# Attention values folded after the sum instead of before it, GpSimd rounding x, and a theta copy by DMA

## The reference, cut to what matters

```python
# B=16 images, C=256 channels, HW=1024 pixels
theta = theta_w @ x                     # 32 rows, 1024 pixels
phi   = pool2(phi_w @ x)                # 2x2 maximum: 32 rows, 256 places
beta  = softmax(theta^T phi, axis=-1)   # 1024 x 256
g     = pool2(g_w @ x)                  # 128 rows, 256 places
o     = o_w @ (g @ beta^T)              # 256 x 1024
y     = gamma * o + x
out   = y + tpl @ y                     # tpl: 27 taps along the channels, circular
```

## Time and profile before

| | |
|---|---|
| Three runs, median | 288.54 us |
| The profiled execution: time, span | 288.93 us, 287.2 us |
| PE busy | 276.3 us (96%) |
| DVE, ACT, POOL busy | 238.0, 235.1, 117.7 us |
| DMA (queue of SP) | 53.1% of 16 engines |
| granted clock, mean | 0.994 |

### The profile page before, as it was taken

The page is one execution under the profiler, slowest core; times in us unless marked ns, Lnnn a source line. Parts: engine busy times, 40 slices in busy tenths (PEclk is TensorE's granted clock), DMA queues, the critical chain, the costliest instruction groups (busy, mean ns, idle before and its releaser), DMA issues.

```text
span 287.2 us, 4324 instructions
## 1 busy us (share of the span) xinstructions
PE 276.3 (96%) x1276; PEld 222.7 (78%) x1276; DVE 238.0 (83%) x401; ACT 235.1 (82%) x519; POOL 117.7 (41%) x59
## 2 busy tenths in 40 slices
PE   5878999999999999999999999999999999999995
PEld 3556778888887888888788888878888887888884
DVE  4897979888897988889798888979888897988750
ACT  1799797997979799797979989797998979799762
POOL 7056336335433633543363353345335334533200
PEclk9799999999999999999999999999999999999999
DMA  7633628193662818466281846628184662818033
GB/s 223 189 53 55 193 119 217 46 243 141 191 193 112 200 71 235 146 192 189 116 224 41 235 146 192 189 118 203 61 238 143 192 189 119 217 46 235 0 149 146
DMA packets 12647, 44.57 MB, mean 155 GB/s; under 512 B 2063, under 2 KB 2653, under 8 KB 11390
## 3 DMA queue, kind: packets, MB, share of 16 engines
q1 hardware_dynamic: 12252, 44.13, 53.1%
q10 hardware_dynamic: 274, 0.20, 0.2%
q0 software_dynamic: 112, 0.13, 0.1%
HBM read 17.37 MB, written 16.78 MB: 119 GB/s over the span
## 4 chain that ended last, share of the span: by engine, by line
PE 87%; DVE 6%; ACT 3%; DMA 2%; issue 1%; POOLq 0%
PE psV L666 15%; PE psV L667 14%; PE psV L668 14%; PE psY L693 10%; PE psY L666 6%; PE psY L667 6%; PE psY L668 6%; PE psV L779 4%; PE psX L746 3%; PE psZ L746 2%; PE psX L732 2%; PE psZ L732 2%; DMA taps_sb<-taps 2%; PE psY L779 1%; DVE theta_aug L513 1%; DVE neg_max L559 1%
## 5 line engine op out<-in xcount | busy, mean ns | idle before, releaser
L324 POOL TENSOR_TENSOR prob_lo<-prob,prob_hi 128x1024 fp32r<-128x1024 f32 x30 | 72.2, 2405 | 94.3 <-ACT prob_hi L396 94.3
L318 POOL TENSOR_TENSOR x_lo<-x_raw,x_hi 128x1024 fp32r<-128x1024 f32 x15 | 36.1, 2409 | 51.5 <-DVE x_hi L490 42.8
L382 ACT ACTIVATE psX<-psX,neg_max 128x256 f32<-128x256 f32 x64 | 28.6, 447 | 25.9 <-DVE neg_max L559 25.7
L369 ACT CAST theta_aug<-thetaphi 32x512 fp32r<-32x512 f32 x64 | 39.6, 618 | 1.2
L666 PE MATMUL psV<-prob_hi,value_hi 128*128 128x512 f32 x94 | 37.8, 403 | 0.0
L668 PE MATMUL psV<-prob_hi,value_lo 128*128 128x512 f32 x94 | 37.2, 395 | 0.0
L667 PE MATMUL psV<-prob_lo,value_hi 128*128 128x512 f32 x94 | 36.9, 393 | 0.0
L507 DVE TENSOR_TENSOR thetaphi<-psY,thetaphi_rest 64x512 f32<-64x512 f32 x32 | 21.8, 683 | 11.4 <-ACT thetaphi_rest L363 11.4
L382 ACT ACTIVATE psZ<-psZ,neg_max 128x256 f32<-128x256 f32 x64 | 29.6, 482 | 0.4 <-DVE neg_max L559 0.4
L513 DVE TENSOR_TENSOR theta_aug<-thetaphi,theta_aug 32x512 fp32r<-32x512 f32 x32 | 26.1, 818 | 1.0
L408 ACT COPY y<-psV 128x512 f32<-128x512 f32 x31 | 18.5, 596 | 9.1 <-PE psV L668 9.1
(11 more groups left out here) (127 smaller groups left out, 723.2 us busy)
## 6 DMA issues: line engine op xcount, KB each, us to landing
x_raw<-x SPq DMA_DIRECT2D x15, 1024.0 KB, 5.5
out<-y SPq DMA_DIRECT2D x15, 1024.0 KB, 4.0
x_edge<-x_hi SPq DMA_DIRECT2D x64, 104.0 KB
x_edge<-x_lo SPq DMA_DIRECT2D x32, 104.0 KB
x_raw<-x SPq DMA_DIRECT2D x4, 256.0 KB, 4.6
out<-y SPq DMA_DIRECT2D x4, 256.0 KB, 2.0
band_rev<-ring SPq DMA_DIRECT2D x2, 128.0 KB, 4.0
proj_raw<-proj_wT ACTq DMA_DIRECT2D x1, 192.0 KB, 3.9
```

What stands on the lines that cost most here:

```text
L318: nc.gpsimd.tensor_tensor(x_lo[:, par, :, cols], x_raw[:, par, :, cols], x_hi[:, par, :, cols].bitcast(F32), ALU.subtract).then_inc(x_lo_r ...
L324: nc.gpsimd.tensor_tensor(prob_lo[:, h], prob[:, h], prob_hi[:, h].bitcast(F32), ALU.subtract).then_inc(prob_lo_ready, 1)
L369: nc.scalar.copy(theta_aug[rows, par, h * HALF:(h + 1) * HALF], thetaphi[0:K, h, :]).then_inc(theta_hi_ready, 1)
L382: last = nc.scalar.activation(tiles[:, t, :], tiles[:, t, :], ACT.Exp, bias=neg_max[:, col:col + 1], accum_out=exp_sum[:, col:col + 1])
```

## The change

For image n, `attention_input(h)` now multiplies the pooled g, turned (g transposed, `gT`), by `prob` into one bank: `o_in` (6 matmuls a half). ACT (half 0) and DVE (half 1) round `o_in` to its high part, DVE makes its low part, and `add_high_attention` and `add_low_attention` multiply by W2's parts (3 matmuls for each of four output banks). g is turned by `g_transposed`: two float32 matmuls of 128 columns against the unit matrix, in place of `values`; ACT and DVE split the result, 256 columns instead of 512. DVE's `split_g` goes. POOL rounds both halves of x. Theta's second high copy is a DMA on SP (`copy_theta_high`), ahead of the x load, and the edge transfers now come behind that load. The taps are fetched by ACT's queue, ahead of the weights, and not by POOL's. Ten idle matmuls stand at the start instead of eight. Banks are reassigned, and with them waits. ("..." marks lines left out.)

```diff
-        g_hi = sb("g_hi", [P, M], F32R)
-        g_lo = sb("g_lo", [P, M], F32R)
-        value_hi = sb("value_hi", [P, 2, MT, C], F32R)
-        value_lo = sb("value_lo", [P, 2, MT, C], F32R)
+        gT_hi = sb("gT_hi", [P, MT, CG], F32R)
+        gT_lo = sb("gT_lo", [P, MT, CG], F32R)
+        o_in_hi = sb("o_in_hi", [P, 2, HALF], F32R)
+        o_in_lo = sb("o_in_lo", [P, 2, HALF], F32R)
...
         psV = ctx.enter_context(nc.psum_tensor("psV", [P, 2, HALF], F32))
         scores_ps = [psX, psZ]
-        thetaphi_ps = [psY[:, 0, :], psY[:, 1, :]]
-        second_thetaphi_ps = [psY[:, 1, :], psY[:, 0, :]]
-        g_ps = [psV[:, 0, :], psY[:, 0, :]]
-        value_ps = psV[:, 1, :]
-        out_ps = [[psV[:, 1, :], psV[:, 0, :]], [psY[:, 1, :], psV[:, 0, :]]]
-        last_out_ps = [out_ps[0], [psY[:, 1, :], psY[:, 0, :]]]
-        w2_ps = psV[:, 1, 0:C]
+        turn_ps = [psV[:, 0, :], psV[:, 1, :]]
+        shared_ps = psY[:, 1, :]
+        g_o_in_ps = psY[:, 0, :]
+        w2_ps = psY[:, 1, 0:C]
...
         def is_second(i, par):
             return is_number(i) and i == 0 and par == 1

-        def thetaphi_bank(i, par, h):
-            return (second_thetaphi_ps if is_second(i, par) else thetaphi_ps)[h]
+        def thetaphi_bank(par, h):
+            return turn_ps[par] if h == 0 else shared_ps
+
+        def g_bank(par, h):
+            return g_o_in_ps if h == 0 else turn_ps[par]
+
+        def gT_bank(i, par):
+            bank = turn_ps[0] if is_first(i, par) else turn_ps[1 - par]
+            return bank[:, 0:M]
+
+        def o_in_bank(i, par, h):
+            if is_last(i, par):
+                return scores_ps[h][:, 0, :]
+            return shared_ps if h == 0 else g_o_in_ps
+
+        def out_bank(i, par, h, f):
+            if f == 0:
+                return turn_ps[par if h == 0 else 1 - par]
+            return g_o_in_ps if h == 1 and is_last(i, par) else shared_ps
...
+            def copy_theta_high(i, par, h):
+                sp.wait_ge(theta_hi_ready, upto(2, i, par, h + 1))
+                cols = slice(h * HALF, (h + 1) * HALF)
+                sp.dma_start(theta_aug[K:2 * K, par, cols].bitcast(F32),
+                             theta_aug[0:K, par, cols].bitcast(F32)).then_inc(theta_copied[h], 16)
...
+            hi, lo = (b[:, :, :].rearrange("p t c -> p (t c)")[:, P:P + CT * P] for b in (band_hi, band_lo))
+            sp.wait_ge(band_parts_ready, 1)
+            stack_edges(edge_w[:, :], edge_w_loaded, (hi, hi))
...
-            stack_edges(edge_w[:, :], edge_w_loaded, (hi, hi, lo))
+            stack_edges(edge_w[:, :], edge_w_loaded, (lo,), 2)
...
                 if has_next(i, par):
-                    x_edges(*following(i, par))
+                    for h in range(2):
+                        copy_theta_high(*following(i, par), h)
...
                     load(i + 1, par)
                 if has_next(i, par):
+                    x_edges(*following(i, par))
...
-            pool.dma_start(taps_sb[:], taps).then_inc(taps_loaded, 16)
...
+            def x_high(i, par, h):
+                cols = slice(h * HALF, (h + 1) * HALF)
+                pool.wait_ge(x_loaded[par], 16 * (i + par))
+                pool.wait_ge(x_used, upto(2, i, par, h - 3))
+                pool.sem_inc(x_buffer_free, 1)
+                nc.gpsimd.tensor_copy(x_hi[:, par, :, cols], x_raw[:, par, :, cols]).then_inc(x_hi_ready[h], 1)
...
-                    for h in range(2):
-                        prob_low(i, par, h)
+                    prob_low(i, par, 0)
+                    pool.wait_ge(theta_lo_ready, upto(2, *following(i, par), 2))
+                    prob_low(i, par, 1)
                 if has_next_but_one(i, par):
+                    x_high(i + 1, par, 0)
                     x_low_of_half_0(i + 1, par)
+                    x_high(i + 1, par, 1)
...
+            act.dma_start(taps_sb[:], taps).then_inc(taps_loaded, 16)
...
-                for rows in (slice(0, K), slice(K, 2 * K)):
-                    nc.scalar.copy(theta_aug[rows, par, h * HALF:(h + 1) * HALF],
-                                   thetaphi[0:K, h, :]).then_inc(theta_hi_ready, 1)
+                cols = slice(h * HALF, (h + 1) * HALF)
+                nc.scalar.copy(theta_aug[0:K, par, cols], thetaphi[0:K, h, :]).then_inc(theta_hi_ready, 1)
+                if is_first(i, par):
+                    nc.scalar.copy(theta_aug[K:2 * K, par, cols], thetaphi[0:K, h, :]).then_inc(first_theta_copy_ready, 1)
...
+            def gT_high(i, par):
+                act.wait_ge(gT_done, upto(1, i, par, 1))
+                nc.scalar.copy(gT_hi[:], gT_bank(i, par).rearrange("p (t c) -> p t c", t=MT)).then_inc(gT_hi_ready, 1)
+
+            def o_in_high(i, par, h):
+                act.wait_ge(o_in_done, upto(2, i, par, h + 1))
+                nc.scalar.copy(o_in_hi[:, h], o_in_bank(i, par, h)).then_inc(o_in_hi_ready[h], 1)
...
+                o_in_high(i, par, 0)
                 if ahead:
                     exp_sums(ni, npar, 0)
+                else:
+                    o_in_high(i, par, 1)
...
                     ln_sums(ni, npar)
+                    gT_high(ni, npar)
                 out_of_psum(i, par, 1, 0)
-                if ahead:
-                    value_high(ni, npar)
-                if has_next_but_one(i, par):
-                    x_high(i + 1, par, 1)
...
-            def x_high(i, par, h):
...
+                pool2(g_pool[:, h * MH:(h + 1) * MH], g_bank(par, h)).then_inc(g_pooled, 1)
+
+            def gT_low(i, par):
+                dve.wait_ge(gT_hi_ready, upto(1, i, par, 1))
+                nc.vector.tensor_tensor(gT_lo[:], gT_bank(i, par).rearrange("p (t c) -> p t c", t=MT),
+                                        gT_hi[:].bitcast(F32), ALU.subtract).then_inc(gT_lo_ready, 1)
+
+            def o_in_high(i, par, h):
+                dve.wait_ge(o_in_done, upto(2, i, par, h + 1))
+                nc.vector.tensor_copy(o_in_hi[:, h], o_in_bank(i, par, h)).then_inc(o_in_hi_ready[h], 1)
+
+            def o_in_low(i, par, h):
+                dve.wait_ge(o_in_hi_ready[h], upto(1, i, par, 1))
+                nc.vector.tensor_tensor(o_in_lo[:, h], o_in_bank(i, par, h), o_in_hi[:, h].bitcast(F32),
+                                        ALU.subtract).then_inc(o_in_lo_ready[h], 1)
...
-                if has_next_but_one(i, par):
-                    x_high(i + 1, par, 0)
+                o_in_high(i, par, 1)
+                o_in_low(i, par, 1)
                 shifts(ni, npar)
+                gT_low(ni, npar)
...
+            def g_transposed(i, par):
+
+                if not is_first(i, par):
                     pe.wait_ge(out_evacuated[0][0], upto(1, i, par, 0))
-                pe.wait_ge(g_lo_ready, upto(1, i, par, 1))
+                pe.wait_ge(g_pooled, upto(2, i, par, 2))
                 for t in range(MT):
                     tile = slice(t * P, (t + 1) * P)
-                    last = three(value_ps[:, t * C:(t + 1) * C], (g_hi[:, tile], g_lo[:, tile]),
-                                 (w2_hi[:], w2_lo[:]), True, True)
-                last.then_inc(value_done, 1)
+                    last = nc.tensor.matmul(gT_bank(i, par)[:, tile], g_pool[:, tile], ident[:], start=True, stop=True)
+                last.then_inc(gT_done, 1)
...
+                    pe.wait_ge(theta_copied[h], 16 * upto(1, i, par, 0))
...
-                    pe.wait_ge(value_lo_ready, upto(1, i, par, 1))
+                    pe.wait_ge(gT_lo_ready, 1)
+                elif (h, f) == (0, 0):
+                    pe.wait_ge(out_evacuated[1][0], upto(1, i, par, 0))
                 elif (h, f) == (0, 1):
                     if has_next(i, par):
-                        pe.wait_ge(g_pooled, upto(2, *following(i, par), 1))
+                        pe.wait_ge(o_in_lo_ready[0], upto(1, i, par, 1))
...
                     if has_next(i, par):
-                        pe.wait_ge(thetaphi_summed, upto(2, *following(i, par), 1 if is_first(i, par) else 2))
+                        pe.wait_ge(g_pooled, upto(2, *following(i, par), 2))
...
+            def attention_input(i, par, h):
+
+                if h == 0 and has_next(i, par):
+                    pe.wait_ge(thetaphi_summed, upto(2, *following(i, par), 2))
+                elif has_next(i, par):
+                    pe.wait_ge(g_pooled, upto(2, *following(i, par), 1))
+                bank = o_in_bank(i, par, h)
+                pe.wait_ge(gT_lo_ready, upto(1, i, par, 1))
+                pe.wait_ge(prob_hi_ready, upto(2, i, par, h + 1))
+                for t in range(MT):
+                    for g_part in (gT_hi, gT_lo):
+                        nc.tensor.matmul(bank, g_part[:, t, :], prob_hi[:, h, t, :],
+                                         start=t == 0 and g_part is gT_hi, stop=False)
                 pe.wait_ge(prob_lo_ready, upto(2, i, par, h + 1))
+                for t in range(MT):
```

(67 more changed lines are left out.)

115 lines of the change are left out of this document (49 added, 66 removed).

## The result

The changed kernel takes 291.25 us (median of 7 runs, 290.07 to 293.21), the kernel before, on the same chip, 288.6 (7 runs, 288.28 to 289.33). The ratio is 1.0093, 95% interval 1.007 to 1.0116: slower, by more than the 0.3% that can be told. The forecast was 290.1 with a range of 286.6 to 293.0, and slower was given 0.55. The profiled execution took 291.25, with a span of 289.3 (before: 288.93 and 287.2).

What follows compares the result with a forecast made beforehand. PE's work bounded the kernel before; DVE's path to `o_in_low` was to set the changed body. 288.93 - 1.9 (start) + 0.2 (first body) + 3.3 (middle) = 290.5, less 0.39 for the median: 290.1 us, range 286.6 to 293.0.

Steps and rivals of the forecast that it cites:

- The middle: Each of 14 bodies: PE waits for DVE's `o_in_low`; body 16.97 us, 0.23 more than before, 3.3 in all; chance 0.52.
- if PE shows no idle time in the middle: Sign that the prediction is wrong: it expected PE idle ahead of the filter group, ending with DVE's `o_in_low`.
- What was late next: End of a body: shift rows ready at 16.6 to 17.0, level with PE's coming at 16.97 and next to be late.
- Turning g: Two float32 matmuls of 128 columns on PE in each body: 0.43 us, at most 0.88.
- What is hidden: Work off PE in each body: ACT's and DVE's changes, the theta transfer and POOL's rounding were to cost no time.
- The theta transfer: Theta's second high copy by DMA: 2.1 us, landing before the scores; rival at 4.0 is late, 299 us, chance 0.06.
- POOL's rounding: Rounding of x on POOL: 1.1 us, hidden up to 2.0; rival that it takes 2.4, 294.3 us, chance 0.07.
- The first body: First body, 16.04 us before: the longer DVE queue makes it 0.2 longer.
- The last: Last body: same number of matmuls, new waits inside other work, so a change of 0.
- The start: Work ahead of the middle: weights, maximum and PE clock together 1.9 us earlier (0.9 to 2.4).
- the weights' 1.2: Start: weights split 1.2 us earlier with the taps first on ACT's queue, 0.5 if they take the taps' 4.6.
- The maximum moved ahead: Start: the maximum of psZ goes ahead of a pooling, so the exponential no longer waits for it: 0.4 us.

Runs made afterwards that it cites:

- e1: The changed kernel with two high additions of `o_in` put between the two halves' scores on PE: 286.34 us, ratio 0.9923.
- e7: The changed kernel with DVE's pooling of g moved from ahead of theta's first low part to between the two maxima: 287.15 us, ratio 0.9937.
- e2: The changed kernel with `o_in_low` of half 0 put ahead of theta's second low part on DVE: 300.21 us, ratio 1.0401.
- e9: The changed kernel with DVE's pooling of g moved behind `o_in_low` and ahead of both maxima: 291.2 us, ratio 1.0088.
- e4: The kernel before with only the start's edits, taps first on ACT's queue and ten idle matmuls: 288.24 us, ratio 0.9982.
- e10: e1 with the pooling of g also moved between the two maxima, as in e7: 284.15 us, ratio 0.9856.
- e3: The changed kernel with theta's second high copy made by ACT again in place of the DMA: 298.31 us, ratio 1.0333.
- e6: e1 with x's high parts rounded by DVE (half 0) and ACT (half 1) again, not by POOL: 286.77 us, ratio 0.9933.

## Why the prediction was right, point by point

**The middle: right, for the reason given.** The body was put at 16.97 and is 16.94; the filter group at 9.35 and it starts at 9.32 (149.42 - 140.10); the psZ scores at 8.6, and they start at 8.64; theta's first low part at 6.1 with 0.68, and it stands at 6.07 with 0.68. The three experiments on this path moved the body as its terms say: cover (e1, 16.65), a shorter queue (e7, 16.66), theta's low part behind `o_in_low` (e2, 17.43). With both repairs the body is 16.47, which is the sum that the prediction gave for PE alone, and 0.27 less than before. So the arithmetic of the change does save what was computed, 14 x 0.27 = 3.8 us, and in the order in which it came a wait of 0.47 a body took it all and 2.8 more. Two things it had wrong. One of its signs of being wrong, "if PE shows no idle time in the middle", came true by its words: PE's rows show none there, only the distances and the weight loads do, so it was the sign that was badly chosen. And it left out 0.08 ahead of the psX scores, which changed nothing, since the psZ scores wait behind them.

**What was late next: right.** Shift rows were forecast ready at 16.6 to 17.0 and are at 16.79 (156.89 - 140.10), and e9 shows their chain as the next bound, at its shift matmul.

**Turning g: right.** Two float32 matmuls take 0.36 to the next start (0.43 forecast), and the matmul behind them another 0.09 (154.52 to 154.84 is 0.32 and not 0.23). Together 0.45.

**What is hidden: right.** The theta transfer lands in 2.0 (2.1 taken), and no wait of PE is put down to it. POOL's rounding is 1.04 (1.1 taken), under the 2.0 from which it would have decided. The Trainium skill's page "GPSIMD Engine Reference", section 4.1, says that GpSimd is roughly at line rate with one input and about twice as slow as VectorE with two; the estimate from it was about 1 us, and the trace agrees with both (2.41 for the subtraction, 1.23 for one of the same size on DVE). The Trainium skill's page "SBUF — State Buffer", section "Who interferes with whom", says that a VectorE instruction with two SBUF inputs contends with a GpSimd one that reads SBUF. The trace agrees, and here it worked in the change's favour: the pooling moved theta's first low part behind POOL's subtraction (0.68 at 146.17, behind POOL's end at 145.99). In the kernel before and in e7 it starts while POOL's runs, takes 0.96 to 0.98, and ends 0.54 to 0.56 behind POOL's end in every body. POOL had started first each time; the other order is in no run.

**The first body: right**, +0.18 (+0.2). **The last: small miss**, about +0.12 (0). The first three output copies start later and the last one at 10.46 of the body as before, so the four stores are issued within 2.38 us and not 4.53; that this makes the end later isn't shown.

**The start: the term that was mis-sized.** "Together 1.9 earlier (0.9 to 2.4)", and it was 1.03; e4 alone gave 0.78. Of the weights' 1.2 only 0.38 came: their transfer took 4.6 from its issue at 1.39, not 3.9, which the prediction had as its other end. Behind them stood a limit that the prediction has no term for: ACT waited for two x tiles, 0.91 and 0.45, and the landing of the second, at 8.92, sets the start. The chain that ended last begins

```profile
2.21 6.71 DMA x_raw<-x
```

Up to the first scores (14.91, 15.35 before) weights and clock together gave 0.44, where 1.5 had been taken. The maximum moved ahead did give its part: psZ's exponential starts at 18.31 without a wait, 19.27 before, 0.52 more. In this profile the clock didn't fall in 9 to 12 us any more, but a gap of 2.19 us now stands ahead of the scores, and in e7, e9 and e10 it falls behind that gap. Seven other profiles have the same start code (e1 to e3, e6, e7, e9, e10): their first body starts between 21.55 and 22.53, 0.7 to 1.7 earlier than before, and none at the forecast 21.3. Nor are ten idle matmuls a cure: in e6 the projections from 8.29 to 11.28 again stand 0.43 apart, the pitch of the lower level, though its granted clock reads 1.00 there; what holds them is open.

**The sum.** 0.87 short in the start, 0.47 too much in the middle, 0.02 in the first body, 0.12 in the last and 0.22 outside the span (1.95, 1.73 before): 0.87 - 0.47 - 0.02 + 0.12 + 0.22 = 0.72, from 290.53 to 291.25. The forecast of the median took off another 0.39, by which the profiled execution of before was above its runs; that of the changed kernel is at its own median. Three figures of the prediction don't come out of its own terms: 14 x 0.23 is 3.2 and not 3.3, its upper end 14 x 0.32 is 4.5 and not 4.8, and the start at its best with the body as before is 286.3 and not 286.6. None decides anything here.

## What to carry to other kernels

A change that saves work on the engine that bounds the kernel saves nothing if the same change hangs that engine on a longer queue; write down for each new wait where the releaser stands in its own queue, from its first input that can't come sooner. When PE's rows show no idle, compare the distances of starts with the same group elsewhere: 0.5 us a body was hidden in "busy 100%". The repair is then mostly an order: something ready put ahead of the wait, and instructions that nobody waits for put behind those that somebody does, but not ahead of the next chain (e7 against e9). Of the two moves of work to idle engines, the theta copy by DMA was worth some 7 us in this order (e3), and POOL's rounding nothing beside e1 (e6): what a move brings depends on whose queue somebody waits for.

## What was not expected of the hardware

- The granted clock of PE falls in the start in some executions of the same start code and not in others. The two windows from 15 to 19 us, of e1 and of e9 (the clock is the third number from the end), follow the same idle time ahead of the scores, 2.28 and 2.29 us. At the lower level (1.2 GHz) W2's four matmuls take 1.91 (e9) and not 1.02 to 1.03. Why it falls in one and not in the other is open.

```profile
15.00:19.00 4.00, 4.00 (x20) 3.15 (x20) 3.96 (x7) 3.73 (x15) 3.76 (x2) 1.00 0.37 63
```
```profile
15.00:19.00 4.00, 4.00 (x14) 3.21 (x13) 3.44 (x6) 3.63 (x16) 3.53 (x2) 0.59 0.54 80
```

- A copy of 27 elements on DVE took 1.06 us (3.75) while POOL's affine select ran, from 3.66 to 4.77; before, behind POOL's work, the same copy took 0.16. The two copies ahead of it, of 13 elements, started at 3.60 and 3.67 and took 0.15. In e4 the second of them started at 3.68 and took 1.09, to POOL's end at 4.74, and the copy of 27 behind it 0.16. So it isn't the copy but when it starts: the one that meets the select ends with it. Here it cost nothing at once, since DVE was idle for 1.06 behind it.
- A matmul group behind a wait of a tenth or two loses another tenth at its first matmul (149.42 to 149.76 is 0.34 and not 0.23; in e7, behind a wait of a tenth, 0.34 too).
